# Causal attention on eight cores: the row maxima computed between the projection matmuls

## The reference

```python
qkv = einsum('btc,oc->bto', x, w_qkv)            # 3 x 16 heads x 64
attn = einsum('bhqd,bhkd->bhqk', q, k) * 64**-0.5
attn = where(causal, attn, -inf)
a = clip(attn, -100, 100)
e = exp(a - max(a, axis=-1))                     # the row maxima
p = e / (sum(e) + 1e-6);  p = p + 1e-8;  p = p / sum(p)
out = einsum('bhqk,bhkd->bhqd', p, v)            # then times w_proj
```

## Time and profile before

| | us |
|---|---|
| median of 2 runs (2071.84, 2095.19) | 2083.52 |
| profiled execution, device time | 2070.88 |
| its span on the slowest core (core 4) | 2069.2 |
| spans of the 8 cores | 2055.7 to 2069.2 |
| granted TensorE clock, mean of the span | 0.626 to 0.631 |

### The profile page before, as it was taken

The page is one execution under the profiler, slowest core; times in us unless marked ns, Lnnn a source line. Parts: engine busy times, 40 slices in busy tenths (PEclk is TensorE's granted clock), DMA queues, the critical chain, the costliest instruction groups (busy, mean ns, idle before and its releaser), DMA issues.

```text
span 2069.2 us, 15991 instructions; the slowest of 8 cores (2055.7 to 2069.2 us)
## 1 busy us (share of the span) xinstructions
PE 1424.5 (69%) x4468; PEld 460.3 (22%) x4504; DVE 691.8 (33%) x1105; ACT 607.7 (29%) x740; POOL 19.4 (1%) x46
## 2 busy tenths in 40 slices
PE   0798766777777677677676777767767509559962
PEld 0343311211222122122121122212212103123420
DVE  2200065334334334333343433424411125441046
ACT  0122101232233232332323223223234202355560
POOL 0000000000000000000000000000000000000000
PEclk9999965555555555555555555555555559679985
DMA  7400010000000000000000000000000382000003
GB/s 245 161 1 0 1 36 1 1 10 11 0 11 11 0 11 0 11 11 0 11 0 11 11 0 11 11 1 11 0 16 0 115 261 62 0 0 1 1 1 162
DMA packets 23668, 62.45 MB, mean 30 GB/s; under 512 B 2208, under 2 KB 15520, under 8 KB 18976
## 3 DMA queue, kind: packets, MB, share of 16 engines
q1 hardware_dynamic: 20864, 52.52, 7.5%
q0 software_dynamic: 2720, 8.92, 1.9%
HBM read 44.06 MB, written 8.39 MB: 25 GB/s over the span
## 4 chain that ended last, share of the span: by engine, by line
PE 61%; DVE 15%; ACT 10%; DMA 6%; issue 6%; DVEq 0%; ACTq 0%; PEldq 0%; SPq 0%; PEld 0%
PE PS L490 13%; PE PS L525 10%; PE PS L406 8%; DVE mx_sb L436 8%; ACT pt L505 7%; PE PS L308 5%; PE PS L558 5%; PE PS L765 3%; PE PS L327 3%; PE PS L835 3%; PE PS L817 3%; PE PS L417 2%; DVE x_f L728 2%; DVE x_f L732 2%; PE PS L553 2%
## 5 line engine op out<-in xcount | busy, mean ns | idle before, releaser
L436 DVE TENSOR_REDUCE mx_sb<-PS 128x1 f32<-128x512 f32 (+3 forms) x576 | 359.7, 624 | 427.2 <-PE PS L406 264.0
L490 PE MATMUL PS<-qs,ks 65*128 65x512 bf16 (+3 forms) x640 | 319.1, 549 | 193.6 <-ACT pt L505 171.6
L505 ACT ACTIVATE pt<-PS 128x1024 bf16<-128x1024 f32 (+3 forms) x256 | 241.7, 944 | 629.1 <-PE PS L490 628.9
L406 PE MATMUL PS<-kp,qp 64*128 64x512 bf16 (+3 forms) x640 | 275.5, 527 | 156.8 <-DVE mx_sb L436 119.9
L525 PE MATMUL PS<-pt,vT_all 128*65 128x512 bf16 (+3 forms) x640 | 276.0, 565 | 13.9 <-ACT pt L512 13.9
L490 PEld LDWEIGHTS PS<-qs,ks 65*128 65x128 bf16 x640 | 72.5, 121 | 424.1 <-issue 423.7
L308 PE MATMUL PS<-x_bf,wqk_bf 128*128 128x512 bf16 x502 | 114.4, 386 | 65.4 <-DVE wqk_bf L286 64.9
L562 DVE COPY ba_sb<-PS 64x512 f32<-64x512 f32 x64 | 43.7, 683 | 340.2 <-PE PS L558 339.5
L406 PEld LDWEIGHTS PS<-kp,qp 64*128 64x128 bf16 x640 | 54.9, 101 | 438.6 <-issue 428.3
L525 PEld LDWEIGHTS PS<-pt,vT_all 128*65 128x65 bf16 x640 | 99.6, 172 | 81.7 <-issue 69.4
L558 PE MATMUL PS<-alpha,ones_rowf 1*64 1x512 f32 x128 | 117.6, 1018 | 0.0
(11 more groups left out here) (81 smaller groups left out, 940.3 us busy)
## 6 DMA issues: line engine op xcount, KB each, us to landing
stgB<-xT SPq DMA_DIRECT2D x8, 1024.0 KB, 6.1
stgB<-wqkT SPq DMA_DIRECT2D x8, 1024.0 KB, 6.0
x_f<-xT SPq DMA_DIRECT2D x8, 1024.0 KB, 7.2
out<-x_f SPq DMA_DIRECT2D x8, 1024.0 KB, 3.9
stgD<-U SPq DMA_DIRECT2D x5, 1024.0 KB, 7.3
stgD<-V SPq DMA_DIRECT2D x5, 1024.0 KB, 5.8
qs<-qp POOLq DMA_DIRECT2D x17, 256.0 KB, 3.7
ks<-kp POOLq DMA_DIRECT2D x17, 256.0 KB, 2.9
```

The source lines that it names most:

```text
L406: prow=prow: e.matmul(PS0[:, lo:lo + w], q_pairs[p2][prow:prow + 64, 128 * i:128 * i + 128], k_pairs[p2][prow:prow + 64, a:a + w], start=T ...
L436: e.reduce_max(mx_sb[:, xcol:xcol + 1], PS0[:, lo:lo + w], axis=AX.X),
L490: cpos=cpos: e.matmul(PS0[:, lo:lo + w], k_stage[hb][:, 128 * j:128 * j + 128], q_stage[qb4][:, cpos:cpos + w], start=True, stop=True),
L505: e.activation(pt[:, cpos - q0:cpos - q0 + span], PS0[:, 0:span], AF.Exp),
```

## The change

- Loading: the cast moves from VectorE to ScalarE, and the tiles of x and of the q/k weights alternate.
- The slots of the q/k projection go pair by pair (q, then k). A slot is computed in two halves of 1024 columns: the first into banks 0 and 1 of PS0, the second into banks 0 and 1 of PS1, each drained by an activation of 1024 columns.
- Banks 2 and 3 of PS0 and of PS1 now hold the scores for the row maxima: PS0 for the even head, PS1 for the odd one. A piece is up to 1024 columns: 24 pieces and 8 combining jobs for a pair. The maxima of all pairs are kept in `m_all` (128 x 256).
- The jobs of a pair enter a list once its k is projected. Behind each half slot, and behind each half of a v tile, `pump(4)` takes up to four of them; what is left runs behind the v tiles.
- v tiles alternate between PS0 and PS1, and the column sums of v (L341) come in a loop of their own behind the rest.
- Attention loses all jobs; `emit_plumb` stays where it was.

```diff
@@ load_cast
-        p.op("vector",
-             lambda e: e.tensor_copy(dst[:, off:off + n], s[:, 0:n]),
+        p.op("scalar",
+             lambda e: e.activation(dst[:, off:off + n], s[:, 0:n], AF.Copy),
              reads=[skey], writes=[dstkey])
@@ loading
     for cc in range(NCC):
         load_cast(x_bf, ("xbf", cc), cc * T,
                   i_x[128 * cc:128 * cc + 128, :], T, stgB)
-    for cc in range(NCC):
         load_cast(wqk_bf, ("wqk", cc), cc * 2048,
                   i_wqk[128 * cc:128 * cc + 128, :], 2048, stgB)
@@ projections
+    def pump(n):
+        for _ in range(n):
+            if strip_q:
+                strip_q.pop(0)()
+
+    def strip_jobs_B(p2):
+        jobs = []
+        for i in range(NTT):
+            kend = 128 * (i + 1)
+            npc = (kend + 1023) // 1024
+            for cb in range(npc):
+                a = 1024 * cb
+                w = min(a + 1024, kend) - a
+                diag = (cb == npc - 1)
+                def piece(a=a, w=w, i=i, cb=cb, npc=npc, diag=diag, p2=p2):
+                    for s0 in range(0, w, 512):
+                        sw = min(s0 + 512, w) - s0
+                        for hh in range(2):
+                            prow = 64 * hh
+                            p.op("tensor", lambda e, ...: e.matmul(
+                                    PSX[hh][:, 1024 + s0:1024 + s0 + sw],
+                                    q_pairs[p2][prow:prow + 64,
+                                                128 * i:128 * i + 128],
+                                    k_pairs[p2][prow:prow + 64,
+                                                a + s0:a + s0 + sw],
+                                    start=True, stop=True),
+                                 reads=[("q", p2), ("k", p2)],
+                                 writes=[(PSN[hh], 2 + s0 // 512)])
+                    if diag:
+                        doff = w - 128
+                        for hh in range(2):
+                            p.op("tensor", lambda e, hh=hh, doff=doff:
+                                 e.matmul(
+                                    PSX[hh][:, 1024 + doff:1024 + doff + 128],
+                                    I_bf[:, :], M_TL[:, :], start=False, ...),
+                                 reads=[("Ibf",), ("MTL",)],
+                                 writes=[(PSN[hh], 2 + doff // 512)])
+                    for hh in range(2):
+                        rd = [(PSN[hh], 2 + b) for b in range((w + 511) // 512)]
+                        ... reduce_max(PSX[hh][:, 1024:1024 + w]) on vector,
+                        ... into m_all (npc == 1) or mx_sb
+                jobs.append(piece)
+            if npc > 1:
+                ... jobs.append(comb)     # two reduce_max, mx_sb to m_all
+        return jobs
+
+    for sl in range(16):
+        pair, is_q = sl // 2, (sl % 2 == 0)
+        woff = 128 * pair if is_q else 1024 + 128 * pair
+        for hf in range(2):
+            PSn, PS = PSN[hf], PSX[hf]
+            for n4 in (0, 1):
+                nn = 2 * hf + n4
+                for cc in range(NCC):
+                    ... matmul into PS[:, 512 * n4:512 * n4 + 512]
+            p.op("scalar", ... activation(dstt[:, 1024 * hf:1024 * hf + 1024],
+                              PS[:, 0:1024], AF.Copy, scale=scl),
+                 reads=[(PSn, 0), (PSn, 1)], writes=[dkey])
+            pump(4)
+        if not is_q:
+            strip_q.extend(strip_jobs_B(pair))
@@ v projection
     for tt in range(NTT):
-        lo = 1024 * (tt % 2)
-        for cc in range(NCC):
-            for hf in range(2):
+        PSn, PS = PSN[tt % 2], PSX[tt % 2]
+        for hf in range(2):
+            for cc in range(NCC):
                 ... matmul
+            pump(4)
         ... drain on scalar, writes=[("vT", tt)]
+    while strip_q:
+        strip_q.pop(0)()
+    for tt in range(NTT):
         for a, b in ((0, 512), (512, 1024), (1024, 1040)):
             p.op("tensor", lambda e, tt=tt, a=a, b=b: e.matmul(
                 PS1[0:1, a:b], ones_col[:, :],
@@ attention
-    for jb in strip_jobs(0):
-        jb()
     emit_plumb(0)
@@ in the loop over heads and blocks
-            if p2n < H // 2 and 1 <= j:
-                quota = 2 if j <= 12 else 0
-                for _ in range(quota):
-                    if jpos[0] < (26 if h % 2 == 0 else 52):
-                        jobs[jpos[0]]()
-                        jpos[0] += 1
@@ behind the second head of a pair
-            while jpos[0] < 52:
-                jobs[jpos[0]]()
-                jpos[0] += 1
             emit_plumb(p2n)
```

More of the change, by code:

```diff
@@ L266, in build_nc @@
     vt8_sb = alloc(grpQKV, "vt8_sb", [1, 1040], BF16, side="right")
+    m_all = alloc(grpQKV, "m_all", [128, 256], F32, side="right")
+    mx_sb = alloc(grpQKV, "mx_sb", [128, 8], F32, side="right")
     grpB = ExitStack()
@@ L298, in build_nc @@
                   2048, stgB)
[L300 to L305, removed]
-            for cc in range(NCC):
[L307 to L313, removed]
+    PSX = (PS0, PS1)
@@ L323, in build_nc @@
     for tt in range(NTT):
-        lo = 1024 * (tt % 2)
-        for cc in range(NCC):
-            for hf in range(2):
-                p.op("tensor", lambda e, lo=lo, cc=cc, hf=hf, tt=tt: e.matmul(
-                    PS0[:, lo + 512 * hf:lo + 512 * hf + 512],
+        PSn, PS = PSN[tt % 2], PSX[tt % 2]
+        for hf in range(2):
+            for cc in range(NCC):
+                p.op("tensor", lambda e, PS=PS, cc=cc, hf=hf, tt=tt: e.matmul(
+                    PS[:, 512 * hf:512 * hf + 512],
                     x_bf[:, cc * T + 128 * tt:cc * T + 128 * tt + 128],
@@ L373, in build_nc @@
              writes=[("ks1", i)])
-    sp_ctr = [0]
     def emit_staging(h):
@@ L387, in emit_staging @@
               reads=[("k", pair)], writes=[("ks0", hb)])
[L389 to L428, removed]
-                                 e.reduce_max(m_sb[:, mcol:mcol + 1],
-                                              PS0[:, lo:lo + w], axis=AX.X,
-                                              negate=True),
-                                 reads=[("P0", bank)], writes=[("msb",)])
-                        else:
-                            xcol = 4 * hh + cb
-                            p.op("vector", lambda e, lo=lo, w=w, xcol=xcol:
-                                 e.reduce_max(mx_sb[:, xcol:xcol + 1],
-                                              PS0[:, lo:lo + w], axis=AX.X),
-                                 reads=[("P0", bank)], writes=[("mxsb",)])
-                jobs.append(piece)
-            if dcb > 0:
-                def comb(e=None, i=i, dcb=dcb):
-                    for hh in range(2):
-                        mcol = 16 * hh + i
-                        x0 = 4 * hh
-                        p.op("vector", lambda e, mcol=mcol, x0=x0, n=dcb + 1:
-                             e.reduce_max(m_sb[:, mcol:mcol + 1],
-                                          mx_sb[:, x0:x0 + n], axis=AX.X,
-                                          negate=True),
-                             reads=[("mxsb",)], writes=[("msb",)])
-                jobs.append(comb)
-        return jobs
@@ L571, in build_nc @@
     emit_staging(1)
-    for jb in strip_jobs(0):
-        jb()
     emit_plumb(0)
-    jobs = []
     for h in range(H):
@@ L579, in build_nc @@
             emit_staging(nxt)
-        p2n = h // 2 + 1
-        if h % 2 == 0 and p2n < H // 2:
-            jobs = strip_jobs(p2n)
-            jpos = [0]
         for j in range(NTT):
@@ L611, in build_nc @@
         emit_epi_piece(h, 2)
-        if h % 2 == 1 and p2n < H // 2:
-            while jpos[0] < 52:
-                jobs[jpos[0]]()
-                jpos[0] += 1
-            emit_plumb(p2n)
+        if h % 2 == 1 and h // 2 + 1 < H // 2:
+            emit_plumb(h // 2 + 1)
     emit_epi_piece(H - 1, 3)
```

58 lines of the change are left out of this document (47 added, 11 removed).

## The result

| | before | after |
|---|---|---|
| median, us | 2072.3 (10 runs) | 2152.6 (12 runs) |
| ratio | | 1.035, 95% interval 1.0307 to 1.0393 |
| span of the profiled execution, slowest core | 2069.2 | 2151.2 |
| plumb activation of pair 0 | 341.4 | 772.1 |
| plumb activation of pair 7 | 1514.7 | 1594.2 |

The kernel is 3.5% slower. The ratio is that of the mean times, without the executions in a slower state in which the cores of one die show a lower granted clock, so it differs a little from the quotient of the medians (1.039).

What follows compares the result with a forecast made beforehand. Attention hid next to nothing of VectorE's row maxima (421 us). Moving them takes 348 us from attention but puts pair 0's plumb 563 us later, at 904.5: +215 on 2070.9 gives 2286 us, range 2160 to 2365.

Steps and rivals of the forecast that it cites:

- What leaves attention: Attention: seven pairs each lose 49.7 us of row maxima, 348 us less in all; a pair without maxima takes 117.9 us.
- The pieces: Row maxima: 48 reductions and 16 combinations a pair instead of 72 and 24; a reduction of 1024 columns takes 1225 ns.
- How they are queued: Pumps: issue order makes VectorE idle before each piece; a pump holds TensorE 7.0 us at 1.2 GHz, 6.0 at 2.4.
- The period: Projection stage: one projection group of 5.7 us plus a mostly cold pump of 6.8, 12.5 us; 60 of them 750 us.
- the range given: Whole kernel: 2160 to 2365 us, reaching to the cold clock and two thirds of the way to the warm one.
- The clock: Projection stage: falls to 1.2 GHz in nearly every pump, returns inside the next group after 4.6 us.
- The rest: Projection stage outside the periods: first slots end at 98.5, left-over jobs 34, column sums 15, drain and barrier 4, plumb wait 3 us.
- The rivals: Whole kernel: cold clock 2364 us (0.10), warm clock 2103 (0.09), hidden fills 2016 (0.04), attention giving back less 2424 (0.02).
- The one in which the clock stays up: Projection stage: 60 periods of 9.45 us, 567 us, 183 less than forecast: 2103 us, +1.5%; chance 0.09.
- the fills are hidden inside a pump: Pumps: the two heads' places work as a double buffer; periods of 8.0 us, 270 less, 2016 us; chance 0.04.
- The forecast's own range: Projection stage: periods of 11 to 13.5 us, giving 2196 to 2346 us; the forecast has chance 0.75.

## Why the prediction was wrong, by its own steps

**What leaves attention: right.** -348 us forecast, 351 measured; pairs of 117.4 us at a clock of about 0.5 (117.9 forecast).

**The pieces: right.** A reduction of 1024 columns takes 1225 ns, as forecast. A slip without effect: a pair had 80 reductions before the change (40 pieces for two heads), not 72.

**How they are queued: right.** The gaps were 0.79 and 1.37 us (0.78 and 1.44 forecast), and the run with head 0 first took 38 us less where this reasoning gave 36 and 8.

**The period: wrong, by a miscount.** The forecast took the same 12.5 us for all 60 pumps. But in the v stage a pump stands behind each half of a tile, so behind 8 matmuls and not 16; the diff says so. This is the step that failed, and the largest part of the error. A v group took 3.2 us on the mean, not 5.7, and the 32 periods 9.75 us each, (716.65 - 414.31)/31. That is 88 us of the 132 by which the plumb of pair 0 came earlier than forecast (772.1 against 904.5): 80 from the groups and 8 from shorter pumps. With the group at its measured 3.2 us and all else left alone, the sum would have been 2286 - 32 x 2.5 = 2206, inside the range given. At the forecast's own price, eight cold matmuls of 0.427 us, it would have been 2286 - 32 x 2.3 = 2212. So the miscount alone doesn't put the time below the range; smaller errors, nearly all to the same side, did the rest.

**The clock: right in kind, a little too dark in the q/k slots.** The two slots without pumps ended at 100.6 us (the 48 matmuls at 90.97 end at 104.07, and the last 16 of them, of 3.45 us, belong to the first period). So the 28 periods took (414.3 - 100.6)/28 = 11.2 us, not 12.5: groups of 4.9 us instead of 5.7, pumps of 6.3 instead of 6.8. The clock was taken to fall in nearly every pump, but five of the six pumps of about 4 us in these slots were followed by a group of 3.45 us, at 2.4 GHz throughout. These are 36 us. That it fell elsewhere is borne out by the groups of 4.5 us and more, and the run with extra matmuls shows its price. The rule cited from the Trainium skill (TensorE: Matmul & The Clock Gate, "Why this matters for your kernels"), taken by itself, would have kept 2.4 GHz. The trace disagrees: the granted clock was 0.80 and 0.66 in two stages in which TensorE never idled longer than 1.7 us at a time (the longest wait of L327 above).

**The rest.** Loading and the two slots without pumps ended at 100.6, not 98.5; the wait for ScalarE's queue came as forecast, to 91 us instead of 89. The left-over jobs took 34.8 us (34 forecast); the sums, the drain, the barrier and the wait of the plumb took 11, not 22. All together: -88 - 36 + 2 - 10 = -132, which is all of it. One reading was off, too: TensorE did not do nothing in the 1.9 us between two v groups before the change. It idled 1.3 to 1.4 us and ran the three small matmuls; the sum doesn't depend on it.

**The rivals.** The one in which the clock stays up named 2103, but its sum had the same miscount; with groups of 8 it would be 2103 - 32 x 1.7 = 2048, 25 less than the 2073 of the run that held the clock near 0.95 and paid for it with extra matmuls. That the fills are hidden inside a pump did not happen. The forecast's own range came from the period's price alone, 11 to 13.5 us; nothing in it, and no rival, allowed for a mistake of counting in a term that enters 60 times.

## What to carry to other kernels

Where a sum is periods times a price, read off the diff what each loop puts into one period, for each loop by itself, before pricing it; two stages that look alike may have half the work between their pauses. Moving work into another engine's stream is worth what the in-order queue leaves of it: put the part that frees a buffer first, and spread the pieces singly, not in blocks. And when TensorE waits often and shortly, price the clock as well as the wait, and try a few throwaway matmuls in the wait before anything larger; too many take the place of the work that the wait was for.

## What the runs showed of the hardware

- Extra matmuls, whose results are thrown away, made the kernel faster, 2153 to 2073 us, by raising the granted clock of the projection stage from 0.80 and 0.66 to 0.96 and 0.94. In attention they brought a pair from 117.8 to 106.0 us (clock 0.52 to 0.70).
- TensorE busy 85 to 89% by its own record doesn't mean that the clock is granted: it was 0.95, 0.74 and 0.58 in stretches with 16, about 11 and 8 full-array matmuls for four jobs. No run here varied the kind of matmul alone, so what in the mix makes the difference stays open.
